# One side job to a key tile, a power ahead of a split, and inverse sums kept in their PSUM bank

## The reference

```python
x = x + head_attention(layernorm(x), ctx, masks, Wq, bq, Wk, bk, Wv, bv)   # 16 heads of 16 channels, over 512 positions
x = x + ffn(layernorm(x), w1, w2, w3)                                      # weights quantised to 4 bits and back, silu gate
x = x + attention(layernorm(x), ctx, wq, wk, wv, wo)                       # one head of 512
x = x + ffn(layernorm(x), w1, w2, w3)                                      # ternary weights, sigmoid gate
```

```python
q = Wq @ target + bq;  k = Wk @ source + bk;  v = Wv @ source + bv         # each (256, 512), split into 16 heads of 16
dot = (q_h.T @ k_h) / 4;  dot = mask * dot - (1 - mask) * 1e6              # (512, 512) per head
amap = softmax(dot) * mask
out_h = amap @ v_h
```

## Time and profile before

| | us |
|---|---|
| median of 3 runs | 1444.24 (1442.85 to 1448.8) |
| profiled execution, device time | 1444.01 |
| its span, first to last instruction | 1442.2 |
| busy in the span: TensorE, Vector, ScalarE, GpSimd | 1304.6, 1018.3, 649.0, 297.1 |
| head attention: sequence 0 | 58.32 |
| sequences 1 to 5, each | 58.75 to 58.76 |
| sequence 6 | 58.49 |

### The profile page before, as it was taken

How to read it: one execution, slowest core, us unless ns; L and a number is a source line. 1 busy time by engine, 2 the same in 40 slices (tenths; PEclk the granted TensorE clock), 3 DMA queues, 4 the chain that set the end, 5 groups by cost and what they waited for, 6 DMA issues and landing times.

```text
span 1442.2 us, 23319 instructions
## 1 busy us (share of the span) xinstructions
PE 1304.6 (90%) x9113; PEld 752.4 (52%) x9142; DVE 1018.3 (71%) x1523; ACT 649.0 (45%) x941; POOL 297.1 (21%) x473
## 2 busy tenths in 40 slices
PE   4787868888988988886999989999999999999998
PEld 2343412222222222223768766777777767777776
DVE  8989779889898897884778846644467544575353
ACT  5675537778777877883453111132111221112210
POOL 1008255545465554320000000000000000000000
PEclk9999979999999999997999999999999999999999
DMA  6300222323334323233744301000010000200000
GB/s 196 113 18 16 75 74 86 114 82 107 104 96 144 100 81 93 70 103 105 254 129 148 100 30 59 16 15 1 30 60 2 30 1 15 68 8 30 1 1 30
DMA packets 78039, 101.23 MB, mean 70 GB/s; under 512 B 14680, under 2 KB 51648, under 8 KB 77928
## 3 DMA queue, kind: packets, MB, share of 16 engines
q1 hardware_dynamic: 75879, 99.43, 21.8%
q0 software_dynamic: 2048, 0.27, 0.1%
HBM read 78.07 MB, written 21.34 MB: 69 GB/s over the span
## 4 chain that ended last, share of the span: by engine, by line
PE 41%; DVE 8%; DMA 1%; issue 1%; ACT 1%; POOL 1%; POOLq 0%; DVEq 0%; SPq 0%; ACTq 0%
PE double L1800 13%; PE double L1814 11%; PE double L1826 6%; PE double L1879 3%; PE double L1847 3%; PE double L1836 3%; PE double L1866 1%; PE double L1784 1%; DVE stats L1987 1%; DVE hid L2034 1%; DMA x_early<-scr_x 1%; DVE gate L2032 1%; DMA out_x<-x_early 1%; DVE x_early L2003 1%; POOL rstd L1973 1%
## 5 line engine op out<-in xcount | busy, mean ns | idle before, releaser
L1029 ACT ACTIVATE prob<-level,head_scale 128x512 f32<-128x512 f32 x512 | 318.9, 682 | 91.0 <-PE level L946 90.9
L1390 DVE TENSOR_REDUCE nmx<-level 128x2 f32<-128x1024 f32 x256 | 304.8, 1221 | 56.1 <-PE level L936 55.8
L1912 ACT ACTIVATE th<-double 128x512 f32<-128x512 f32 x96 | 53.9, 562 | 386.3 <-PE double L1800 213.2
L946 PE MATMUL level<-stacks 59*128 59x512 f16 x512 | 174.1, 387 | 24.7 <-ACT prob L1029 24.4
L936 PE MATMUL level<-stacks 57*128 57x512 f16 x512 | 149.9, 392 | 12.2 <-DVE nmx L1390 11.5
L1800 PE MATMUL double<-x_parts,f0w 128*128 128x256 f16 x1408 | 157.6, 275 | 1.6 <-PEq L521 1.6
L374 PE MATMUL level<-prob,x_parts 128*128 128x448 bf16 (+1 forms) x527 | 123.7, 387 | 38.4 <-DVE prob L421 16.9
L1973 POOL TENSOR_TENSOR rstd<-meanvar,halfpow 128x2 f32<-128x2 f32 x22 | 15.2, 691 | 688.5 <-DVE meanvar L1993 688.5
L1800 PE MATMUL double<-x_parts,f1w 128*128 128x256 f16 x1408 | 155.2, 273 | 0.4 <-DVE hid L2034 0.4
L1800 PEld LDWEIGHTS double<-x_parts,f0w 128*128 128x128 bf16 x1408 | 138.9, 99 | 20.6 <-issue 2.2
L1800 PEld LDWEIGHTS double<-x_parts,f1w 128*128 128x128 bf16 x1408 | 137.5, 98 | 18.5 <-DVE hid L2034 0.6
(11 more groups left out here) (254 smaller groups left out, 1873.4 us busy)
## 6 DMA issues: line engine op xcount, KB each, us to landing
stacks<-scr_q SPq DMA_DIRECT2D x64, 96.0 KB
stacks<-scr_k SPq DMA_DIRECT2D x64, 96.0 KB
hid<-in_f1w1t SPq DMA_DIRECT2D x8, 704.0 KB, 6.4
hid<-in_f1w2t SPq DMA_DIRECT2D x8, 704.0 KB, 4.2
inputs<-in_x SPq DMA_DIRECT2D x8, 512.0 KB, 7.2
inputs<-in_ctx SPq DMA_DIRECT2D x8, 512.0 KB, 7.0
scr_q<-splits SPq DMA_DIRECT2D x16, 256.0 KB, 2.4
scr_k<-splits SPq DMA_DIRECT2D x16, 256.0 KB, 2.2
```

Of the source, the lines that this page charges most:

```text
L946: nc.tensor.matmul(pB[n % 2], Ks[rows, g, j // 2, P * c:P * (c + 1)], Qs[rows, g, j // 2, :], start=True, stop=True).then_inc(s["b_pe"], 1)
L1029: nc.scalar.activation(prob[:, c, j, :], pB[(64 * b + 16 * g + 4 * c + j) % 2], ACT.Exp, scale=hscale[:, 10:11]).then_inc(s["exp_done"], 1)
L1390: nc.vector.tensor_reduce(nmx[:, g % 2, :, half, tt], pA[(32 * b + 8 * g + u // 2) % 2], AX.X, ALU.max, negate=True).then_inc(s["max_done" ...
L1912: y = nc.scalar.activation(th[:, 0:m, :], src[:, 0:m, 0:S], ACT.Tanh, scale=0.5 / XS)
```

## The change

Five edits in the head attention.

- The table `MISC` gives each tile at most one side job, in its first half, but for (1,0), which has both o jobs. q0 stays in (0,0), k0 moves from its second half to (0,3). The o jobs move from (0,3) to (1,0). q1 moves from (1,0) to (1,3), k1 from (1,0) to (2,0). v0 stays in (2,3), v1 moves from its second half to (3,0).
- ScalarE's `q_evac`, Vector's `residual` and `v_evac`, and GpSimd's `split` move with them. The evacuations now stand in the middle of the tile of their job.
- GpSimd's `ln_pow` of the norm now stands in front of the split of q1.
- SP issues fill 1 ahead of the store of the second half of q and k.
- `normalise` writes the reciprocals into column 17 of their own bank, and the product with the mask reads them from there. It is a tensor_tensor now.

```diff
         MISC = {
-            (0, 0): [("q", 0, 1), ("k", 0, 1)], (0, 1): [("nm", 1, 0), None], (0, 2): [("t", 3, -1), None],
-            (0, 3): [("o", 0, -1), ("o", 1, -1)],
-            (1, 0): [("q", 1, 1), ("k", 1, 1)], (1, 1): [("nm", 2, 0), None], (1, 2): [("t", 0, 0), None],
-            (2, 1): [("nm", 3, 0), None], (2, 2): [("t", 1, 0), None], (2, 3): [("v", 0, 1), ("v", 1, 1)],
-            (3, 1): [("nm", 0, 1), None], (3, 2): [("t", 2, 0), None],
+            (0, 0): [("q", 0, 1), None], (0, 1): [("nm", 1, 0), None], (0, 2): [("t", 3, -1), None], (0, 3): [("k", 0, 1), None],
+            (1, 0): [("o", 0, -1), ("o", 1, -1)], (1, 1): [("nm", 2, 0), None], (1, 2): [("t", 0, 0), None],
+            (1, 3): [("q", 1, 1), None],
+            (2, 0): [("k", 1, 1), None], (2, 1): [("nm", 3, 0), None], (2, 2): [("t", 1, 0), None], (2, 3): [("v", 0, 1), None],
+            (3, 0): [("v", 1, 1), None], (3, 1): [("nm", 0, 1), None], (3, 2): [("t", 2, 0), None],
         }
+        PROJECTED = {(0, 0): (0, 0), (0, 3): (0, 1), (1, 3): (1, 0), (2, 0): (1, 1)}
...
                 if not last:
+                    fill(b + 1, 1)
                     store_parts(b + 1, 1)
-                    fill(b + 1, 1)
-                if not last:
                     fill(b + 1, 2)
...
                         exps(b, g, c, 0)
-                        if c == 0 and g < 2 and not last:
-                            q_evac(b + 1, g, (0,))
+                        if (g, c) in PROJECTED and not last:
+                            i, n = PROJECTED[g, c]
+                            q_evac(b + 1, i, (n,))
...
                         exps(b, g, c, 1)
-                        if c == 0 and g < 2 and not last:
-                            q_evac(b + 1, g, (1,))
...
                 for g in range(NG):
-                    if not last and g < 2:
-                        split(b + 1, g, (0,))
+                    if not last and g == 0:
+                        split(b + 1, 0, (0,))
+                    if not last and g == 2:
+                        split(b + 1, 1, (1,))
...
-                    if not last and g < 2:
-                        split(b + 1, g, (1,))
                     if g == 1 and not ending:
                         ln_pow(b + 2)
+                    if not last and g < 2:
+                        split(b + 1, g, (1 - g,))
...
-                nc.vector.reciprocal(rs[:], t4[:, :, :, HD]).then_inc(s["t_a"], 1)
+                nc.vector.reciprocal(t4[:, :, :, HD + 1], t4[:, :, :, HD]).then_inc(s["t_a"], 1)
                 dve.wait_ge(s["t_a"], 2 * e + 1)
-                nc.vector.scalar_tensor_tensor(rs[:], rs[:], 1.0, mcol[:, :, b].unsqueeze(2).broadcast_to([P, DK, G]),
-                                               ALU.mult, ALU.mult).then_inc(s["t_a"], 1)
+                nc.vector.tensor_tensor(rs[:], t4[:, :, :, HD + 1], mcol[:, :, b].unsqueeze(2).broadcast_to([P, DK, G]),
+                                        ALU.mult).then_inc(s["t_a"], 1)
...
-                            if g == 0 and c == 3 and not first:
+                            if g == 1 and c == 0 and not first:
                                 residual(b - 1, (half,))
...
-                            if g == 2 and c == 3 and not last:
-                                v_evac(b + 1, half)
+                            if (g, c) in ((2, 3), (3, 0)) and half == 0 and not last:
+                                v_evac(b + 1, g - 2)
```

## The result

The changed kernel takes 1423.0 us (median of 5 runs, 1421.7 to 1424.88) against 1445.51 for the kernel before (5 runs beside it, 1442.85 to 1448.8). The ratio is 0.9842, with a 95% interval from 0.9824 to 0.986: 1.6% faster. The forecast was 1414.4, its range 1406 to 1426. So the time lies in the stated range and the sign is right, but it lies outside the forecast's own range of 1410 to 1420, and of 29.6 us that were to go, about 22 went. The profiled execution took 1422.36 us, its span is 1420.5 (before 1442.2), and the span gives 21.7 us to share out.

A forecast was written before the change was run, and what follows sets the result against it. Head-attention tiles were bound by the chain of scores, exponentials and value matmuls, plus 9.80 us of side jobs and waits per sequence. Gains 22.4 - 1.3 + 5.2 + 3.3 = 29.6 took 1444.0 to 1414.4 us; range 1406 to 1426.

The forecast's parts named there:

- The price of a side job: TensorE's head-attention tiles: first-half jobs cost only what exceeds the idle 0.56 us (q or k 0.42), second-half jobs everything.
- The 0.34 that I gave for q1 and k1 as neighbours: Tile (2,0): ScalarE's exponentials run late behind q1's evacuation, so k1's job there costs 0.34 us more.
- The stall of the small product: Vector's normalise, product of reciprocals and mask: with one PSUM operand no stall, 0.2 us; stall bounds 0 and 1.26.
- The order of GpSimd and SP: Power ahead of q1's split, later k splits, fill 1 ahead of the second store: all costed at nothing.
- rival 3: Tile (1,0) waits for group 1's row of maxima, a transfer becoming the bound: slower, 1454 us; chance 0.03.
- The cover that I called thin: Group 1's row of maxima lands at about 13.1 us into the sequence; tile (1,0) begins at 13.29.
- Sequence 4's late x: x lands 14.8 us into sequence 4, too late for statistics at 13.53: 1.3 us of gain lost.
- Sequence 6: Head attention's sequence without statistics: the 0.73 and 0.27 go, 53.27 us against 58.49, gain 5.2.
- there stand the statistics of the norm, from 13.53, and they take 1.68 until the next maximum: Vector's order ahead of (1,0): the statistics delay o0's residual to 17.02, so o1 waits 0.73 us.
- 1, statistics not in the way: Statistics don't delay o1 on Vector: 0.73 + 0.27 go in six sequences, giving 1409 us; chance 0.06.
- 2, Vector stays late: The bank doesn't cure the product's stall, or L1398 is held: 1428 us, in part 1421; chance 0.10.
- 4: No effect: Vector's order of residuals and maxima gives back what the second halves shed, 1444 us; chance 0.03.

## Why the prediction was right, and where it was off

**The price of a side job, right.** A job in a first half costs what exceeds the idle 0.56 there, in a second half all of it. Every row of the table above but (1,0) agrees within 0.12 us, and the v job moved by itself gave 1.08 a sequence. The 0.34 that I gave for q1 and k1 as neighbours measured 0.27 (3.75 against 3.48), and the two job tiles with a c = 0 tile behind them, (0,3) and (1,3), take 0.07 more than (0,0). That for q1 and k1 this is one effect, part of which has moved from (2,0) into (1,3), is only argued.

**The stall of the small product, right.** No stall in 32 of 32, at 0.17 each (0.2 in the sum). What I didn't see is that the moved splits had cured most of it anyway: the bank alone is worth 10.5 us on the kernel before, and on top of the other edits 1 us by the profiles. One reading went too far: of q's wait of 0.53, which I put down to L1419, the bank alone takes away 0.28. My sum didn't depend on which of the two did it.

**The order of GpSimd and SP, right.** Power, splits, fill 1 and the store cost nothing; no score waits for a transfer, and rival 3 did not occur. The cover that I called thin is thin: in sequence 4 the row of group 1's maxima lands 5.6 us after its issue, 12.6 us into the sequence, 0.8 ahead of tile (1,0). But my price for the power's cover, "rival 3's kind" (1.5 us a sequence), was far too low: a power behind its split costs 4.6 to 5.0 in tile (2,1) alone, and 4.3 to 7.4 a sequence with the lower clock.

**Sequence 4's late x, right.** Vector's timeline there:

```profile
438.04 1.29 DVE L1233 BATCH_NORM_STATS2 st<-inputs 128x6 f32<-128x512 f32 x2 [1.10 <-DMA inputs<-in_x]
```

x lands 14.7 us into the sequence, forecast 14.8. And because the statistics come after k0's split is over there, the addition L1239 takes 170 ns in this one sequence: the minimum of its row. The kernel with the early loads moved, in which x is in time, has 979 ns as its minimum.

**Sequence 6, right.** 53.32 for 53.27.

**The step that was mis-sized: "there stand the statistics of the norm, from 13.53, and they take 1.68 until the next maximum".** They take 2.51. The 1.68 was read in a kernel in which GpSimd had ended k0's split before the statistics began. The change itself moves k0 to (0,3), and so its split beside them. The rest of that chain holds to 0.01: with 0.83 more, the residual ends at 17.85 by my working and at 17.86 in the profile (498.07 less 480.21). o1's wait comes out at 1.44 and not 1.56, since the value matmuls of its tile end 0.12 later than I had them. This is 0.7 us in each of sequences 1, 2, 3 and 5, 2.9 us in all; in sequence 4 the addition isn't held. The two kernels without the addition on Vector give 0.9 a sequence back, and the one with the statistics elsewhere 1.56. I had written that a tensor_scalar on SBUF may still be held and had named L1398 for it. The one that was held lies inside the 1.68 of my own sum.

The Trainium skill, page "SBUF — State Buffer", section "Who interferes with whom", says that a tensor_scalar on SBUF can contend with GpSimd when it runs in a two-port mode, and that whoever issues first holds the shared ports for the whole instruction while the other waits. The trace agrees: the split started first, at 495.16, and ended at 496.32; the addition, 0.17 us when it runs free, started at 495.34 and ended at 496.34. Which mode it ran in no trace shows.

**What no step had: the clock.** In tile (1,1) of sequences 0 and 4 TensorE runs some 3.2 to 3.4 us at its lower level, and the tile takes 5.89 and 4.92. The second profile of the changed kernel has both again, with 5.89 and 4.91. In sequence 0 there are no o jobs; TensorE's timeline there shows what comes ahead of it:

```profile
220.43 0.39 PE L937 MATMUL level<-stacks 57*128 57x512 f16 x2 [0.61 <-DVE nmx L1392]
...
221.98 0.59 PE L901 MATMUL pM<-identb,nmp 128*8 128x128 bf16 x4 [0.96 <-DVE nmp L1402]
```

The first wait, 0.61, is for a maximum that stood behind the held addition; with the epsilon on GpSimd it is gone, nm's 0.96 stays, the clock stays at its upper level, and (1,1) takes 3.50. The sequence then takes 55.06 (55.02 was forecast). The other profiles say the same: this tile takes 5.37 to 5.89 in all six with the held addition, and 3.27 to 3.50 in the four in which the addition isn't held. So in sequence 0 the missing 2.2 us hang on the held addition, most of them by way of the clock. In sequence 4, (1,1) has 1.4 more than forecast, which is the missing 1.3; there the stretch also occurs without the addition, and also without the late load's extra wait. It does not occur with GpSimd's epsilon, though that kernel waits 1.78 for the residual there. And sequence 5 of the changed kernel, with TensorE busy for 1.38 of the 3.70 us ahead of the same point (496.5 to 500.2), keeps the upper level, while sequence 0, busy for 2.41 of 3.70 (218.0 to 221.7), loses it. Which idle time brings the clock down is therefore open. The start of sequence 0 varies as well: its first two tiles take 8.60 in this profile and 10.97 in the second one of the same kernel, where their granted clock is 0.50.

**Accounts.** Of the 7.9 us by which the gain in the span falls short of the forecast: 2.9 in sequences 1, 2, 3 and 5 (the addition), 2.2 in sequence 0 (the addition and the clock), 1.3 in sequence 4 (the clock), 0.45 ahead of the first tile, and 1.3 in the dense part, where one more short stretch runs at the lower clock (710.0 to 713.4); sequence 7 gives 0.2 back. The last three are no more than profiles differ by among themselves: the first column score comes at 198.9 to 201.6 us, and the stretch from sequence 7 on varies by 4.7.

**The rivals.** 1, statistics not in the way: wrong, they made all of the wait. 2, Vector stays late: the nearest to the truth in kind, since an instruction on Vector was held by GpSimd, and its partial form was priced at 1421; it was another instruction at another place. 3 and 4 did not occur. That the time still lies in the stated range is in part luck: the range had been widened for rivals 1 and 2, and what took up the room, the held epsilon addition and the clock, stood in neither.

## What to carry to other kernels

When a job is moved, look at what it triggers on the other engines, and read again every duration in the sum that may now run beside it: a minimum from the old profile is a duration with the old neighbours. For Vector and GpSimd, list every instruction that can be held by the other, down to the smallest, and move the whole group (here the statistics, by two tiles) rather than the single instruction. And measure two cures for one stall apart and together, since whichever is applied second is worth little.

## What the runs showed of the hardware

- An addition on 128x2 elements took 0.99 to 1.00 us in five of six cases beside a GpSimd split of 1.16 us, and 0.17 to 0.18 when free. It ended with the split each time, so the price was what was left of the split and not the instruction's own size. Two applications of the norm took 1.94 to 2.40 us where the power stood behind the split of q1, 1.20 in the changed kernel and 1.00 in the kernel before.
- Reciprocal and product through PSUM cost hardly more than through SBUF: the product takes 174 ns from either, the reciprocal 256 into PSUM and 248 into SBUF (medians).
- Two waits of TensorE close together, 0.61 and 0.96 us in sequence 0, 1.86 and 0.95 in sequence 4, were followed by some 3.3 us at 1.2 GHz, which cost 2.4 and 1.5 us. Waits of 1.44 and 0.95 in four other sequences were not, and waits of 1.42 and 0.96 in sequence 4, with the early loads moved, were. In sequence 0 a wait of 0.61 so cost more than its length; when it does could not be told.
